# Second attention of an early-fusion kernel: when Pool fills the stacks with zeros

## What is computed

```python
def _layernorm(x, axis=-1, eps=1e-05):
    m = jnp.mean(x, axis=axis, keepdims=True)
    v = jnp.var(x, axis=axis, keepdims=True)
    return (x - m) / jnp.sqrt(v + eps)
...
h = h + _L0_attn_ref(_layernorm(h), ...)
h = h + _L0_ffn_ref(_layernorm(h), ...)     # 8 experts and a shared one
h = h + _L1_attn_ref(_layernorm(h), ...)    # the second attention
h = h + _L1_ffn_ref(_layernorm(h), ...)

def _L1_attn_ref(x, Wq, bq, Wk, bk, Wv, bv, Wo, bo):   # H=16 heads, G=4 groups, HD=16
    q = (x @ Wq.T + bq).reshape(b, n, G, hpg, HD)
    k = (x @ Wk.T + bk).reshape(b, n, G, HD)
    v = (x @ Wv.T + bv).reshape(b, n, G, HD)
    scores = jnp.einsum('bqghd,bkgd->bghqk', q, k) * scale
    attn = jax.nn.softmax(scores, axis=-1)
    y = jnp.einsum('bghqk,bkgd->bqghd', attn, v).reshape(b, n, d)
    return y @ Wo.T + bo
```

## Time and profile before

| | us |
|---|---|
| median of 3 runs | 864.26 |
| lowest and highest | 863.16, 865.48 |
| the profiled execution's own time | 865.68 |
| its span, first to last instruction | 863.8 |
| TensorE busy | 744.2 |
| VectorE busy | 602.8 |
| ScalarE busy | 338.9 |
| Pool busy | 145.2 |

### The profile page before, as it was taken

One profiled execution on the slowest core, in us unless ns is written; L12 is line 12 of the kernel. 1 busy time (PEld: TensorE's weight loads), 2 busy tenths in 40 slices (PEclk: granted clock), 3 DMA queues, 4 the chain that ended last, 5 costly groups with the idle time before them and its releaser, 6 DMA issues.

```text
span 863.8 us, 14418 instructions
## 1 busy us (share of the span) xinstructions
PE 744.2 (86%) x4818; PEld 631.2 (73%) x4818; DVE 602.8 (70%) x1361; ACT 338.9 (39%) x595; POOL 145.2 (17%) x132
## 2 busy tenths in 40 slices
PE   4548996899999997347999999999847899999997
PEld 4538994699999996235666655553635899999997
DVE  6396667677777777827767767772787777777776
ACT  1305543433333333101766656668134233333332
POOL 0105552000000000436113320211253000000000
PEclk9999996999999999556999999999977999999999
DMA  7300000000000000054353444421400000000000
GB/s 242 124 41 1 1 0 0 1 2 1 1 1 1 0 0 0 1 93 94 72 104 87 98 80 104 90 44 22 185 0 1 1 19 1 19 19 2 20 19 19
DMA packets 21559, 34.77 MB, mean 40 GB/s; under 512 B 6572, under 2 KB 17500, under 8 KB 20960
## 3 DMA queue, kind: packets, MB, share of 16 engines
q1 hardware_dynamic: 16632, 31.60, 13.9%
q10 hardware_dynamic: 4872, 2.46, 1.5%
HBM read 24.03 MB, written 9.99 MB: 39 GB/s over the span
## 4 chain that ended last, share of the span: by engine, by line
PE 75%; DVE 14%; issue 3%; ACT 3%; DMA 3%; SPq 1%; POOL 1%; ACTq 0%; DVEq 0%; POOLq 0%
PE PS L1232 16%; PE PS L1234 16%; PE PS L1233 15%; PE PS L1534 6%; PE PS L1473 6%; PE PS L1491 4%; DVE MX L1133 2%; PE PS L1261 2%; DVE xnp L854 1%; PE PS L1354 1%; PE PS L1563 1%; PE PS L1320 1%; DVE stats L845 1%; DMA KS<-scrH 1%; PE PS L1240 1%
## 5 line engine op out<-in xcount | busy, mean ns | idle before, releaser
L1133 DVE TENSOR_REDUCE MX<-PS 128x1 f32<-128x288 f32 x288 | 125.1, 452 | 50.7 <-PE PS L1473 47.2
L1065 DVE SCALAR_TENSOR_TENSOR h<-PS,cmb,h 128x256 f32<-128x256 f32 (+1 forms) x342 | 143.8, 476 | 0.3 <-PE PS L1234 0.3
L662 ACT ACTIVATE PR<-PS 96x768 f32<-96x768 f32 x144 | 115.3, 806 | 47.2 <-PE PS L1491 45.1
L630 ACT ACTIVATE sg<-PS 128x384 f32<-128x384 f32 x114 | 56.0, 491 | 165.7 <-PE PS L1234 165.7
L1473 PE MATMUL PS<-KS,QS 96*128 96x288 f32 x288 | 97.7, 358 | 17.3 <-DMA KS<-scrH 15.2
L1050 DVE TENSOR_TENSOR al<-aa,ah 128x384 fp32r<-128x384 f32 x114 | 63.6, 558 | 67.2 <-ACT ah L634 67.2
L1473 PEld LDWEIGHTS PS<-KS,QS 96*128 96x128 f32 x288 | 57.2, 202 | 59.1 <-DVE MX L1133 39.3
L634 ACT ACTIVATE ah<-aa 128x384 fp32r<-128x384 f32 x114 | 60.0, 527 | 84.1 <-DVE aa L1044 84.1
L1044 DVE TENSOR_TENSOR aa<-sg,PS 128x384 f32<-128x384 f32 x114 | 63.3, 555 | 26.4 <-ACT sg L630 25.8
L1234 PE MATMUL PS<-xTl,W1h 128*128 128x384 f32 x240 | 81.0, 337 | 0.0
L1232 PE MATMUL PS<-xTh,W1h 128*128 128x384 f32 x240 | 80.8, 337 | 0.0
(11 more groups left out here) (232 smaller groups left out, 1557.9 us busy)
## 6 DMA issues: line engine op xcount, KB each, us to landing
QS<-scrH SPq DMA_DIRECT2D x32, 144.0 KB, 3.9
W1raw<-in_w SPq DMA_DIRECT2D x1, 3840.0 KB, 11.7
W0raw<-in_w SPq DMA_DIRECT2D x1, 3456.0 KB, 10.7
scrH<-qh SPq DMA_DIRECT2D x8, 432.0 KB, 2.5
scrL<-ql SPq DMA_DIRECT2D x8, 432.0 KB, 3.3
QS<-scrL SPq DMA_DIRECT2D x16, 144.0 KB, 4.5
out_tokens<-h SPq DMA_DIRECT2D x6, 384.0 KB, 2.3
x_in<-in_x SPq DMA_DIRECT2D x2, 1024.0 KB, 6.3
```

The costliest lines, as they stand in the source:

```text
L662: A_(PR[0:KT, c0:c0 + 2, :], PS[0:KT, b:b + 2, 0:CW], ACT.Exp).then_inc(s["e_exp"], 1)
L1065: ins = V.scalar_tensor_tensor(out=hj, in0=PS[:, b + t // 2, (t % 2) * D:(t % 2) * D + D], scalar=cmb[:, ds(g * GT + t, 1), e:e + 1].squee ...
L1133: V.tensor_reduce(MX[:, c // NSH, c % NSH:c % NSH + 1], PS[:, max_bank(it, c), 0:POS], AX_X, ALU.max).then_inc(s["e_mx"], 1)
```

## The change

On Pool, the wait for `e_xn` moves from its place ahead of the bias additions to a place ahead of the two `zeros`. With it, the four fills of `QS` and `KS` start when VectorE has normalised all six groups, and no longer when the last expert's result has been added. The fills of `neg1` and `MX` stay where they were. The other engines' programs are unchanged.

```diff
@@ -451,6 +451,7 @@
             own.settle()
             pool.sem_inc(s["e_const"], 1)
 
+        pool.wait_ge(s["e_xn"], NG)
         zeros(0)
         zeros(1)
 
@@ -477,7 +478,6 @@
         pool.sem_inc(s["e_const"], 1)
         low_halves(1, 1)
 
-        pool.wait_ge(s["e_xn"], NG)
         with pool.Fori(0, NT) as j:
```

## The result

| | before | after |
|---|---|---|
| median, us | 864.37 (15 runs) | 860.52 (15 runs) |
| lowest and highest, us | 863.16, 868.97 | 857.24, 862.85 |
| ratio of the times, 95% interval | | 0.9942 (0.9925 to 0.9959) |
| profiled execution, span, us | 863.8 | 860.1 |

The ratio is that of the means, 860.21 against 865.22: 5.0 us less, between 3.5 and 6.5. The medians alone say 3.9 us. The single times of either kernel lie up to 6 us apart, so the interval is the better guide.

A forecast was written before the change was run, and what follows sets the result against it. It took the second preparation's serial chain to be bound by VectorE instructions held inside Pool's fills. 8.0 us of stall, less 2.4 waiting for Pool, gives 5.6; 864.26 - 5.6 = 858.7 us, range 856.2 to 861.4.

The forecast's parts named there:

- The stall goes: Second preparation, VectorE: L756 and L761 no longer held by Pool's fills, group 2 normalised at 347.6, 8.0 us sooner.
- the rival in which they stay long: L756 and L761 are not long because of the fills; low halves 2.4 us later, 866.7 us, chance 0.03.
- The preparation keeps its pace: Second preparation: the last group is still normalised 6.45 us after group 2, so at 354.1.
- Fills 10.1 us, free at 364.2: Pool: the four moved fills run behind the last normalising, from 354.1 to 364.2 or 364.3.
- the rival that a fill holds them too, in part or to the end: Fills also hold L939 and L1143: in part 861.2 us, chance 0.06; to the end 864.8 us, chance 0.04.
- Low halves to 366.6, gain 5.6: Pool, first image: three low halves queue behind the fills, ending at 366.6 instead of 372.18; 2.4 of 8.0 us lost.
- SyncE and the later fills are hidden: SyncE's waits for the fills and Pool's VA, recb and last PR fills, 5.6 us earlier, cost nothing.
- TensorE's clock: Lower level (0.50) kept in the sum; up to 2.2 or 2.5 us less if higher, 1.5 us allowed if later.
- the rival of an early clock: TensorE's clock comes up sooner because its idle gap shrinks by 8.0 us: up to 2.5 us more, 856.2 us, chance 0.10.
- Everything behind moves as one block: Behind the split, DMAs start by semaphores, so the 5.6 us gain is kept to the end.

The follow-up runs named there:

- split fills: Changed kernel, but the second pair of fills (QS1, KS1) goes behind the low halves of image 0: 0.9898 of the kernel before.
- e2: Kernel before, fills in place, with L756 and L761 written as scalar_tensor_tensor with two SBUF inputs: 1.0000 of the kernel before.
- e4: Changed kernel, but QS0 and KS0 are filled at once after the FFN; only QS1 and KS1 wait for the normalising: 0.9972 of the kernel before.
- e5: Kernel before, fills in place, with L756, L761 and the second preparation's normalising (L854) written with two SBUF inputs: 0.9940 of the kernel before.
- after_again: The changed kernel measured once more with no edit: 0.9949 of the kernel before.
- e3: Changed kernel with one more fill of QS0 at the head of the moved fills: 0.9997 of the kernel before.
- e6: On split fills, third preparation: two Pool weight splits ahead of the first root, one behind the first normalised group, three behind the last: 0.9801 of the kernel before.

## Why the prediction was right, point by point

- *The stall goes, 8.0 us.* Group 2 was to be normalised at 347.6, and was at 347.41, in an execution that was 0.23 us ahead at this place. L756 and L761 took 0.17 us, so the rival in which they stay long is out. By itself the term is 8.00 us in the kernel with split fills. Its cause was argued from ends that coincide and from the first preparation; the kernels with fills left in the old place (e2, e4, e5) showed it.
- *The preparation keeps its pace.* Last group at 353.86 (354.1 forecast), 6.45 us behind group 2, as before.
- *Fills 10.1 us, free at 364.2.* 10.02 us, to 363.94. L939 and L1143 were not held; the rival that a fill holds them too, in part or to the end, is out.
- *Low halves to 366.6, gain 5.6.* 366.42, gain 5.53. The 2.4 us for Pool's queue are shown from both sides: taken off (split fills) they come back, and one more fill costs 3.99 for 3.94.
- *SyncE and the later fills are hidden.* The first stack out is at 366.51, 0.09 us after the last low half. The fill of `PR` ended at 372.47, ahead of the first maximum. That came at 377.95 where 377.9 was forecast, but 0.23 us of it are the head start: counted from L444 the gain is 5.35 us there.
- *TensorE's clock.* It stayed at 0.50 all through the shorter gap, a transposed group took 1.54 us as before, so there the rival of an early clock is out. After the first scores a small part of it came: the clock rose between 383 and 384 us, 5.7 us behind the first maximum against 7.2 before, and at the stack out of image 1 the gain is 0.4 us larger. The other profiles fit: after_again and e3 have 5.0 and 6.5 us, and 0.5 and 0.4 us more at image 1; in the remaining five the clock rises 6.8 to 7.5 us behind the first maximum, and the gain at image 1 differs by 0.2 us at most. That the clock gives these tenths is read from this agreement; no run isolates it.
- *Everything behind moves as one block.* Right in the mechanism: of the eight kernels six keep their local gain to within 0.9 us up to L393 (two lose more, the changed kernel 2.0 and e2 1.1, both with a wait of TensorE for the late stack, of 1.1 and 0.7 us), and from there to the end all take within 0.7 us of the 258.2 us of before, but for after_again (261.6) and e6, which changes that part. In the total the forecast is 1.8 us too low: 858.7 against 860.52, and the medians lie 3.9 us apart, the means 5.0. The median of three runs held (864.26, 864.37 with 15). The spread did not: it was taken as 2.3 us, and either kernel shows some 6 with 15 runs. The two profiles of the changed kernel lost 2.0 and 0.8 us up to L393, and the second 3.4 more behind it, as told above; what the unprofiled executions lost, and whether the kernel before loses as much, is not shown. The measured time is inside the range, and 5.6 us (0.9935) inside the interval of the ratio, so the terms are well tested by the profiles and the total only loosely by the time.
- *Slips that cost nothing.* By its own terms the later fills end at 372.6, not 372.7, and one transposed group at the upper clock saves 0.67 us, not 0.6. Its rows on the clock leave out that in the kernel before the clock stood at the upper level between the last projection and the first scores (1.00 from 371 to 373 us) and fell again before they began.

## What to carry to other kernels

A tiny VectorE instruction with a long record and nothing to wait for is a wait: look what Pool does in the same microseconds, and whether their ends coincide. Then there are three cures, all measured here: Pool's work behind the critical stretch, cut to the part that is needed first (0.9898); VectorE's instruction in a form with two SBUF inputs, if Pool only writes (0.9940 with Pool's work left where it was, and nothing gained, 1.0000, while the normalising kept its held form); and the same look at every other place where the two meet (0.9801). When Pool's work is moved, ask what stands behind it on Pool: here 2.4 of 8.0 us went there.

## What the runs showed that was not expected

- A break between two pairs of fills let about one held instruction through, so that freeing L756 and L761 alone gained nothing (8.71 us for three L854). Why L756 and the first L854 sit through `QS` and `KS` of the first pair, up to the break, while in the second pair VectorE gets in between `QS` and `KS` (release at 354.04 and at 353.9, and that `KS` took 1.21 or 1.20 instead of 1.05 us), stays open.
- The largest loss of this kind was not at the place of the change but in the third preparation, where three groups took 6.2, 8.8 and 2.8 us instead of 1.05 each.
- Beside Pool's last three splits in e6 another VectorE instruction with two SBUF inputs (L997, the first of its line) took 2.42 us; in the kernel before (L994, no split beside it) it took 0.31.
